# Two transformer layers on one core: the last part taken slot by slot, side work threaded through the attention, fewer filler products

## What is computed

```python
h = _layernorm(x) * (1 + ca) + sa
x = x + ga * _L0_attn_ref(h, ...)     # test-time training: a recurrence over 32 chunks
h = _layernorm(x) * (1 + cb) + sb
x = x + gb * (gelu(h @ U1 @ V1 + b1) @ U2 @ V2 + b2)
h = _layernorm(x) * (1 + ca) + sa
q, k, v = split(h @ w_attn.T)         # 16 heads of 16, window of 64 and 4 global tokens
x = x + ga * (softmax(mask(q k.T / 4)) @ v) @ w_proj.T
h = _layernorm(x) * (1 + cb) + sb     # xr, xk: h mixed with the token before it, by mu
x = x + gb * sigmoid(xr @ W_r.T) * (relu(xk @ W_k.T) ** 2 @ W_v.T)
```

## Time and profile before

| | us |
|---|---|
| median of 3 runs | 2469.89 |
| lowest, highest | 2457.07, 2473.36 |
| the profiled execution, its own time | 2457.74 |
| its span | 2456.0 |
| busy in the span: PE, DVE, ACT, POOL | 2143.7, 1602.1, 1558.3, 1100.0 |

### The profile page before, as it was taken

One profiled execution on the slowest core, in us unless ns is written; L12 is line 12 of the kernel. 1 busy time (PEld: TensorE's weight loads), 2 busy tenths in 40 slices (PEclk: granted clock), 3 DMA queues, 4 the chain that ended last, 5 costly groups with the idle time before them and its releaser, 6 DMA issues.

```text
span 2456.0 us, 88067 instructions
## 1 busy us (share of the span) xinstructions
PE 2143.7 (87%) x32669; PEld 1375.5 (56%) x32669; DVE 1602.1 (65%) x3901; ACT 1558.3 (63%) x4121; POOL 1100.0 (45%) x1221
## 2 busy tenths in 40 slices
PE   7999996878888877885699999999999999999898
PEld 4455452555555555553366565665655756657566
DVE  6888885676776776773277474773746847557465
ACT  6788883676676676664365484564845748547474
POOL 1212223676776777776423344234433343233323
PEclk9999998898998898887799999999999999999999
DMA  6655557333334333411421312312123112220120
GB/s 199 179 154 161 175 152 186 69 67 82 77 68 88 79 69 75 87 32 37 134 69 44 91 22 76 78 45 74 38 76 77 45 52 60 74 72 11 33 52 18
DMA packets 387235, 201.37 MB, mean 82 GB/s; under 512 B 257376, under 2 KB 372704, under 8 KB 386800
## 3 DMA queue, kind: packets, MB, share of 16 engines
q1 hardware_dynamic: 386800, 195.65, 30.3%
HBM read 101.67 MB, written 69.27 MB: 70 GB/s over the span
## 4 chain that ended last, share of the span: by engine, by line
PE 44%; DVE 16%; issue 15%; ACT 14%; POOL 7%; SPq 2%; DMA 1%; ACTq 1%; DVEq 1%; POOLq 0%
PE psum L1050 11%; ACT arena L1569 8%; DVE arena L1861 6%; PE psum L1143 4%; PE psum L1102 3%; PE psum L906 3%; PE psum L1110 3%; PE psum L900 3%; ACT arena L1368 2%; POOL arena L1637 2%; PE psum L1216 2%; PE psum L893 2%; PE psum L914 2%; PE psum L1082 2%; PE psum L1179 2%
## 5 line engine op out<-in xcount | busy, mean ns | idle before, releaser
L1795 POOL TENSOR_TENSOR arena<-arena 128x400 f32<-128x400 f32 x256 | 218.3, 853 | 481.9 <-DVE arena L2223 481.9
L1368 ACT ACTIVATE arena<-psum,scan_sb 64x128 f32<-64x128 f32 x1152 | 307.7, 361 | 115.0 <-PE psum L974 107.0
L1569 ACT ACTIVATE arena<-psum,arena 128x100 f32<-128x100 f32 x1024 | 270.0, 367 | 6.4 <-DVE arena L2215 6.3
L1861 DVE SCALAR_TENSOR_TENSOR arena<-psum,taps_sb,arena 128x511 f32<-128x511 f32 (+2 forms) x288 | 212.5, 747 | 55.1 <-ACT arena L1268 48.4
L808 PE MATMUL psum<-arena,w_in_sb 128*128 128x512 f32 x512 | 230.1, 598 | 1.0 <-ACT arena L1261 1.0
L1611 POOL TENSOR_TENSOR arena<-arena 128x512 f32<-128x512 f32 x64 | 80.7, 1273 | 264.5 <-ACT arena L1294 264.5
L900 PE MATMUL psum<-arena 128*32 128x17 f32 x10240 | 127.3, 192 | 80.7 <-issue 60.0
L1940 DVE TENSOR_TENSOR arena<-psum,scan_sb 64x512 f32<-64x512 f32 x290 | 188.5, 673 | 3.3 <-PE psum L1006 2.9
L2215 DVE TENSOR_REDUCE arena<-psum 128x4 f32<-128x400 f32 x256 | 146.3, 573 | 58.5 <-PE psum L1166 48.1
L1561 ACT ACTIVATE arena<-psum 100x512 f32<-100x512 f32 x256 | 156.1, 610 | 42.8 <-PE psum L1179 36.6
L906 PE MATMUL psum<-arena,scan_sb 128*128 128x512 f32 (+1 forms) x328 | 172.3, 612 | 11.1 <-ACT psum L1413 4.5
(11 more groups left out here) (225 smaller groups left out, 4711.7 us busy)
## 6 DMA issues: line engine op xcount, KB each, us to landing
arena<-arena SPq DMA_DIRECT2D x144, 128.0 KB
arena<-x SPq DMA_DIRECT2D x32, 512.0 KB, 4.0
arena<-gates_d SPq DMA_DIRECT2D x112, 128.0 KB, 4.0
v_rows_d<-arena SPq DMA_DIRECT2D x64, 136.0 KB
k_rows_d<-arena SPq DMA_DIRECT2D x64, 136.0 KB
arena<-k_rows_d SPq DMA_DIRECT2D x128, 68.0 KB, 2.1
arena<-v_rows_d SPq DMA_DIRECT2D x128, 68.0 KB, 2.3
v_d<-arena SPq DMA_DIRECT2D x32, 256.0 KB, 4.5
```

Source lines behind the costliest of these rows:

```text
L1368: ins = act.activation(dst.rearrange("p (t x a) -> p t x a", x=PP, a=INNER)[upper, :, x], src.rearrange("p (t a) -> p t a", a=INNER)[upper ...
L1569: act.activation(c_soft[s][:, f % 2, u], sc, ACT.Exp, bias=c_max[s][:, u:u + 1]).then_inc(c_act.mark(f"exp{s}{f}u{u}"), 1)
L1795: pool.tensor_tensor(soft, soft, c_rec[s].unsqueeze(2).broadcast_to([P, 4, KEYS]), ALU.mult).then_inc(c_pool.mark(f"prob{s}{f}"), 1)
L1861: ins = dve.scalar_tensor_tensor(out=a_acc[:, t, j:TOK], in0=bank[2 + t][:, 0:TOK - j], scalar=taps_sb[:, t % KT, col:col + 1], in1=a_acc[ ...
```

## The change

The attention no longer alternates between slots: all 16 frames of slot 0 come first, then those of slot 1. What alternates with the step (buffers, banks) now goes by `t % 2`. So slot 0 needs only its own `q`, `k` and `vt` to start, and is over halfway through. The work that this sets free is placed between the steps by the tables `PE_SIDE`, `ACT_SIDE` and `DVE_SIDE` and the matching `if t == ...`: keys and values of slot 1 (steps 0 to 3), the statistics of the next pair (steps 5 to 19), and `wp`, the residual, the norm, `turn3` and `h3` of slot 0 (steps 16 to 32), as a rule two steps behind what each reads. The tail is reordered in the same way, slot 1 behind slot 0. The `u1` product and its copy `p` move from the start of a pair to the end of the one before. `Sqrt` and DVE's reciprocal become `Ln` and `Exp(-0.5 x)` on ACT, the set of tables is named by hand, and 17 filler products a pair are left (4 + 4 + 4 + 5).

```diff
-        ATT = [(f, s) for f in range(FRAMES) for s in SLOTS]
+        ATT = [(f, s) for s in SLOTS for f in range(FRAMES)]
+        QUARTERS = len(ATT) // QTR
 
         T_LAG, PV_LAG, YE_LAG, Y_LAG = 3, 4, 5, 6
-        WARM = {"s0": 9, "t0": 6, "t1": 4, "pv0": 4, "t2": 2, "pv1": 2, "norm1": 10, "u10": 6, "u11": 6, "norm2": 22, "vt0": 8, "vt1": 6, "norm3": 10, "turn30": 6, "turn31": 8, "pv28": 1, "t29": 1, "pv29": 1, "t30": 2, "pv30": 2, "t31": 2, "pv31": 2}
-        TURNED, Y_BANKS = 2, (3, 6, 7)
-
-        def y_bank(s, quarter):
-
-            return bank[Y_BANKS[(len(SLOTS) * quarter + s) % len(Y_BANKS)]]
+        WARM = {"norm2": 22, "vt0": 4, "pv30": 4, "pv31": 4, "turn31": 5}
+        TURNED, SPARE = 2, 7
+        SCORES = (0, 3)
+
+        def y_bank(quarter):
+
+            return bank[5 + quarter % 2]
...
+        PE_SIDE = {0: ["k10", "k11"], 2: ["vt10", "vt11"], 16: ["wp00"], 23: ["wp01"], 31: ["turn300"]}
+        PE_END = {32: ["turn301", "wp10"]}
+        ACT_SIDE = {0: [f"ks1{g}" for g in range(4)], 2: ["vt10"], 27: ["ln30", "rstd30"], 32: ["h300", "h301"]}
+        DVE_SIDE = {0: [f"ks1{g}" for g in range(4)], 3: ["vt11"], 18: ["x300"], 19: tile_names("st3", 0, (0,)), 20: tile_names("st3", 0, (1,)),
+                    24: ["x301"], 26: tile_names("st3", 0, (2, 3)) + tile_names("ag3", 0, range(TT)), 28: tile_names("xh3", 0, (0, 1)),
+                    29: tile_names("xh3", 0, (2, 3)), 33: ["x310"] + tile_names("st3", 1, (0, 1)), 35: ["d0"], 36: ["xr00"]}
...
+                turn_2(0, (1, 2))
+                stay_warm("vt0", bank[5])
+                pe.wait_ge(c_act.sem, c_act.at(i, "h201"))
+                values(0, (1, 2))
+                if ahead:
+                    pe.wait_ge(n_dve.sem, n_dve.at(i + 1, "x01"))
+                columns(0, "q", (3, 0))
+                if ahead:
+                    pe.wait_ge(n_dve.sem, n_dve.at(i + 1, "x11"))
+                columns(0, "k", (7, 4))
+                turn_2(1, (5, 6))
+                pe.wait_ge(c_act.sem, c_act.at(i, "h211"))
+                columns(1, "q", (5, 6))
...
+                    if t == 16:
+                        pe.wait_ge(c_dve.sem, c_dve.at(i, "y01"))
+                        pe.wait_ge(c_pool.sem, c_pool.at(i, "wp0"))
+                        projected(0, 0, bank[SPARE])
+                    if t == 23:
+                        pe.wait_ge(c_dve.sem, c_dve.at(i, "x300"))
+                        pe.wait_ge(c_dve.sem, c_dve.at(i, "y03"))
+                        projected(0, 1, bank[SPARE])
+                    if t == 31:
+                        pe.wait_ge(c_dve.sem, c_dve.at(i, "xh303"))
+                        turn_half(0, 0, c_pe, "turn3", bank[SPARE])
...
+                    if t >= len(ATT) + 2:
+                        stay_warm(f"pv{t - PV_LAG}", bank[3])
...
+                    if t == 32:
+                        pe.wait_ge(c_act.sem, c_act.at(i, step_name("exp", 30) + f"u{QUADS - 1}"))
+                        turn_half(0, 1, c_pe, "turn3", bank[0])
+                        pe.wait_ge(c_dve.sem, c_dve.at(i, "y11"))
+                        pe.wait_ge(c_pool.sem, c_pool.at(i, "wp1"))
+                        projected(1, 0, bank[1])
+
+                pe.wait_ge(c_dve.sem, c_dve.at(i, "y13"))
+                projected(1, 1, bank[5])
+                receptance(0, (3, 4))
+                stay_warm("turn31", bank[7])
+                pe.wait_ge(c_dve.sem, c_dve.at(i, "xh313"))
+                turn_half(1, 0, c_pe, "turn3", bank[7])
+                turn_half(1, 1, c_pe, "turn3", bank[5])
+                hidden(0, (0, 1))
+                if ahead:
+                    next_turn(i + 1, 0)
+                receptance(1, (5, 7))
+                pe.wait_ge(c_act.sem, c_act.at(i, "kk01"))
+                mixed(0, (0, 1))
+                if ahead:
+                    next_u1(i + 1, 0)
+                    pe.wait_ge(n_act.sem, n_act.at(i + 1, "p0"))
+                hidden(1, (6, 2))
+                if ahead:
+                    pe.wait_ge(c_act.sem, c_act.at(i, "r01"))
+                    next_turn(i + 1, 1)
+                    pe.wait_ge(n_act.sem, n_act.at(i + 1, "h10"))
+                pe.wait_ge(c_act.sem, c_act.at(i, "kk11"))
+                mixed(1, (3, 7))
+                if ahead:
+                    next_u1(i + 1, 1)
...
-                    act.activation(n_std[s], n_mv[s][:, :, 1], ACT.Sqrt, bias=parity[:, 6:7]).then_inc(n_act.mark(f"std{s}"), 1)
+                    act.activation(n_std[s], n_mv[s][:, :, 1], ACT.Ln, bias=parity[:, 6:7]).then_inc(n_act.mark(f"ln{s}"), 1)
+                    act.wait_ge(n_act.sem, n_act.at(n, f"ln{s}"))
+                    act.activation(n_rstd[s], n_std[s], ACT.Exp, scale=-0.5).then_inc(n_act.mark(f"rstd{s}"), 1)
...
+                act.preload_act_table_set("natural_log_exp_and_others")
+                std(2, 0)
+                modulate(2, 0, 0, bank[1])
+                modulate(2, 0, 1, bank[2])
+                std(2, 1)
+                values(0, bank[1])
+                queries(0, bank[3])
+                modulate(2, 1, 0, bank[5])
+                modulate(2, 1, 1, bank[6])
+                keys(0, bank[4])
+                queries(1, bank[5])
...
+                        keys(1, bank[2])
+                    if t == 2:
+                        values(1, bank[5])
+                    if t == 19 and ahead:
+                        next_std(i + 1)
+                    if t == 27:
+                        std(3, 0)
+                    if t == 32:
+                        modulate(3, 0, 0, bank[SPARE])
+                        modulate(3, 0, 1, bank[0])
...
+                std(3, 1)
+                modulate(3, 1, 0, bank[7])
+                modulate(3, 1, 1, bank[5])
+                hidden(0, (0, 1))
                 if ahead:
-                    for s in SLOTS:
-                        act.wait_ge(c_dve.sem, c_dve.at(i, f"xk{s}{KT - 1}"))
-                        if s == 1:
-                            act.wait_ge(c_pool.sem, c_pool.at(i, "d1"))
-                        next_modulate(i + 1, s)
+                    next_modulate(i + 1, 0)
+                receptance(0, (3, 4))
+                if ahead:
+                    next_p(i + 1, 0)
+                receptance(1, (5, 7))
+                hidden(1, (6, 2))
+                if ahead:
+                    act.wait_ge(c_dve.sem, c_dve.at(i, "xk11"))
+                    next_modulate(i + 1, 1)
+                    next_p(i + 1, 1)
...
+                    if t in (5, 6, 7, 8) and ahead:
+                        next_stats(i + 1, 0, (t - 5,))
+                    if t in (11, 12) and ahead:
+                        next_stats(i + 1, 1, (t - 11,))
+                    if t in (14, 15) and ahead:
+                        next_stats(i + 1, 1, (t - 12,))
+                    if t in (10, 16) and ahead:
+                        next_spread(i + 1, t // 16)
...
+                mix(0, 0, "xr", c_xr[0], (1,))
+                residual(3, 1, 1, "wp", bank[5])
+                statistics(3, 1, (2, 3))
+                spread(3, 1)
+                mix(0, 1, "xk", c_xk[0], (0,))
+                normalise(3, 1, range(TT))
+                mix(0, 1, "xk", c_xk[0], (1,))
                 if ahead:
-                    for s in SLOTS:
-                        dve.wait_ge(c_pe.sem, c_pe.at(i, f"turn3{s}{KT - 1}"))
-                        next_normal(i + 1, s)
-                for s in SLOTS:
+                    dve.wait_ge(c_pe.sem, c_pe.at(i, "turn301"))
+                    next_normal(i + 1, 0)
+                shift(1)
+                mix(1, 0, "xr", c_xr[1])
+                mix(1, 1, "xk", c_xk[1])
+                if ahead:
+                    dve.wait_ge(c_pe.sem, c_pe.at(i, "turn311"))
+                    next_normal(i + 1, 1)
```

More of the change, by code:

```diff
@@ L1524, in pair, with hidden @@
+                def hidden(s, banks):
+                    for m in range(KT):
+                        act.wait_ge(c_pe.sem, c_pe.at(i, f"kk{s}{m}"))
+                        act.activation(c_kk[s][:, m], bank[banks[m]], ACT.Relu).then_inc(c_act.mark(f"kk{s}{m}"), 1)
                 for f in range(FT):
@@ L2206, in pair @@
+                spread(2, 1)
+                if ahead:
+                    next_sum(i + 1, 0)
+                normalise(2, 1, range(TT))
+                if ahead:
+                    next_sum(i + 1, 1)
+                values(0, bank[2])
+                queries(0, bank[0])
+                keys(0, bank[7])
+                queries(1, bank[6])
                 quads = lambda t: t.rearrange("p (t k) -> p t k", t=2)
-                for t in range(len(ATT) + Y_LAG + 1):
+                for t in range(len(ATT) + Y_LAG):
```

612 lines of the change are left out of this document (307 added, 305 removed).

## The result

| | kernel before | changed kernel |
|---|---|---|
| median us | 2465.06 (4 runs, 2457.07 to 2473.36) | 2431.93 (4 runs, 2429.12 to 2441.8) |
| ratio, 95% interval | | .987, .983 to .992 |
| the profiled execution, its own time | 2457.74 | 2434.04 |

The account below looks back on a forecast made before the run. In attention a two-step dependency loop, with neither ACT nor PE full, sets the pace; elsewhere work plus waits. A typical pair gives -6.8; 2457.7 - 49.2 (seven pairs) - 11.0 (last) = 2397.5, say 2398 us; range 2366 to 2448.

Parts of the forecast that it names:

- Slot by slot, the second norm to the first scores: Stretch from second norm to first scores: 28.55 before, 18.2 forecast, -10.3 us, of which 6.9 only moves.
- The attention with side work: First scores to scores of step 31: 51.1 before, 59.8 forecast, +8.7 us for 10.4 of moved work.
- the places named: Attention steps 16, 19, 23 and 26 to 29, the only ones expected to depart from 1.6 us.
- All side work: DVE and ACT work between attention steps, costed at 2.5 us a pair: 1.0 for DVE and 1.5 for ACT.
- The branch: ACT's loop branch, 2.1 us idle after `p`, then a table load: +1.6 us a pair at six branches back.
- the clock falls: Rival, 6%: waits behind the attention leave TensorE at 1.2 GHz for half the tail, 17.6 a pair, 2539 us.
- Scores of step 31 to the end of `u1`: The pair's tail: 48.2 before, 35.3 of work and 6.1 of waits, 41.4 forecast, -6.8 us.
- `u1` 2.05: Work term in the tail: `u1` of both slots priced at 2.05 us.
- 1.4 in the last steps, whose chain stays as it was: Wait term in the tail: 1.4 us in the attention's last steps, with eight fillers lying in it.
- slot 1's `r`: Wait term in the tail: 0.8 us before slot 1's `r`, since DVE has other work ahead.
- Table loads at nothing: Table loads fall from six a pair to three; the three that go were credited with no gain.
- The base: The profiled execution before, 2457.7 us, from which the sum started; the median after might lie some microseconds above.

Follow-up runs that it names:

- e7: The changed kernel with six more filler products between the first `v1` and the first `u2`; 2434.0 us, ratio .988.
- e2: The changed kernel with ACT's last part written out for its pairs instead of looped; 2415.1 us, ratio .981.
- e1: The changed kernel with `u1` of both slots side by side at the pair's end and both copies `p` after them; 2408.3 us, ratio .979.
- e13: The changed kernel with slot 0's third normalisation replaced by a reciprocal over 4 columns per tile; 2433.9 us in a single run.
- e12: The changed kernel with slot 0's normalising tiles at steps 28 and 29 placed between maximum and sum on DVE; 2427.2 us, ratio .985.
- e4: The changed kernel without its seventeen filler products a pair (the last pair's 22 stay); 2427.4 us, ratio .985.
- e15: The changed kernel with the edits of e1, e2 and e12, and fillers cut in the drain and re-placed behind it; 2387.6 us, ratio .970.
- e5: The kernel before with `Ln` and `Exp` in place of `Sqrt` and reciprocal, and a table preload ahead of norm 2; 2460.6 us, ratio .998.
- a_again: The changed kernel run once more with nothing edited; 2433.1 us, ratio .990.
- e8: The changed kernel with the second half of slot 0's third normalisation moved behind the last maximum; 2437.3 us, ratio .987.

## Why the prediction was half right

**Slot by slot, the second norm to the first scores: right.** 18.35 for 18.2 in pair 5. PE waits .43 and 1.10 for `h`, where 1.2 each was written, four fillers in the first.

**The attention with side work: right as a stretch** (59.4 for 59.8), in part as its terms offset each other. To step 5 it takes 12.2 for 11.8. Of the later steps, from one product of scores to the next, 16 and 23 take 3.37 with their half of `wp`, 21, 22, 28, 29 and 30 take 1.79 to 2.25, and the others 1.59 to 1.67. Steps 21, 22 and 30 were not among the places named, while 19, 26 and 27, which were, pass at 1.59 to 1.62. In step 21 the two `Ln` and `Exp` of the next pair hold ACT from 2066.11 to 2067.09, and the transposes wait .59 for the copy behind them. All side work from step 5 on costs some 2.2 beside `wp`, where 2.5 was written.

**The branch: right in mechanism, short by the clock.** 30.35 for 30.3 in pair 5, and idle "issue" of 2.1 ahead of the load. The mean is 30.90, since in four of six pairs the clock also fell behind the wait: with their longer idle time taken off, these are 1.1 to 1.6 longer than pair 5, .75 a pair over the seven. With e7's fillers the clock shows no drop and the rest of the wait stays; e2 takes both away, and 2.6 of the stretch with them. This is the rival "the clock falls" in a small place, not in the tail where it was put. The Trainium skill, page Advanced Engine Details and Errata, section Control Flow Timing, gives a compare-and-branch about 0.11 us. The trace has 2.1 of idle time for the whole jump back.

**Scores of step 31 to the end of `u1`, forecast at 48.2 to 41.4: the step that failed.** It measured 44.7. The term "`u1` 2.05" was mis-sized: it is the price of both slots side by side, and the change parts them, so that 1.93 has to stand twice, 1.8 more; e1 gets 2.1 back, .1 of it from a shorter wait for `p`. "1.4 in the last steps, whose chain stays as it was" was too little: the drain is 10.9 for some 8.9. By e13, 1.0 of that is DVE's norm at steps 28 and 29 (e12 gets half of it back by another place). By e4, 1.0 is fillers "that lie in it" (e15 gets .7 back): four of them stand where nothing is waited for, and the other four last .84 where the copy leaves .39. Together that is 3.8; some .5 came back where waits were written too long (slot 1's `r` waits .29, not .8).

**Why the norm is dear there.** Of two normalising tiles, the second, which starts while POOL's product runs, ends only behind it, and so does one of 16 columns; with POOL idle two whole tiles take .73. The Trainium skill, page SBUF — State Buffer, section Who interferes with whom, counts `tensor_scalar` among the instructions of VectorE that can take a port pair shared with GpSimd, and says that whoever issues first has it for its whole instruction while the other is blocked. The traces agree: the second tile takes .94 beside the product and .41 without, and the product, issued while the first tile runs, .97 and .93 against .85.

**Table loads at nothing: right** for the two of the three that e5 takes away; the third was not tried alone.

**The base.** Seven pairs gave 24.4 and the last 8.7 (155.8 to 147.1), 33.1 together. Ahead of the first pair, from the first `wo` product to the first `v1`, the changed kernel takes 1.3 more (25.8 against 24.5), with `u1` parted there too, so the last part gave 31.8; the medians differ by 33.1, and by 28.2 in the rounds of a_again. The sum was written on the profiled execution, and the two profiled ones differ by 23.7 only. Of the 36 missing there, 23 are the last stretch (7 x 3.3), 6 the first stretch, 2 the last pair, 1.3 the start, and 8 the later start of part three, which no line of the change explains; some 4 came back elsewhere. The execution that the sum was written on was 7.3 faster than the median, probably because its second part had ended early (1177.7; in e5, with the same parts one and two, 1189.9 in an execution of 2470.4). The others were not profiled. The forecast said that the median might lie above, and moved the number by half a microsecond only.

What stays open: when the clock falls behind the branch (TensorE idle for 2.09 in pair 6, with a drop, and for 2.46 in pair 3, without), and why the second part of a run ends up to 22 us apart with the same instructions. No run changes the order of the slots alone, so its share in the gain is read from the stretches only.

## What to carry over

Before you take a group of products apart, look whether its halves ran side by side; a price read from a joint row holds for the joint row alone. An idle wait that the sum prices at its own length may cost the clock behind it, so fill it, but no further than it lasts. A timing experiment by leaving work out has to take away the instruction's claim on a shared resource too, not its columns alone.

## What was not expected of the hardware

- Products of 64 output columns for each slot, written to different halves of the partitions, ran in 1.95 for both, 1.93 for one.
- ScalarE's jump back in the loop was 1.57 to 2.53 of idle time (e1, e8); straight code for seven pairs showed none.
- DVE's tile of 16 columns took .83 to .87 where it started beside POOL's product, .26 to .29 where it started ahead of it.
